# A four-layer diffusion block on one core: two top-k steps moved from VectorE to ScalarE and GpSimd, Newton steps of three instructions, projections at half pace in some phases

## What is computed

```python
scores = jnp.einsum('bqhd,bkhd->bhqk', q, k) / jnp.sqrt(jnp.float32(D))
top_s, top_i = jax.lax.top_k(scores, TOPK)          # TOPK = 16 of 77 keys
attn = jax.nn.softmax(top_s, axis=-1)
vg = jnp.take_along_axis(v_bh[:, :, None, :, :], top_i[..., None], axis=3)
o = jnp.einsum('bhqk,bhqkd->bqhd', attn, vg).reshape(B, L, C)
```

## Time and profile before

| what | value |
|---|---|
| median of 3 runs | 2932.87 us (2932.09 to 2951.3) |
| the profiled execution's own time | 2946.59 us |
| its span, first to last instruction | 2945.2 us |
| PE, PEld busy | 2444.7 us (83%), 1246.7 us |
| DVE busy | 1811.3 us (62%) |
| ACT busy | 1253.7 us (43%) |
| POOL busy | 258.6 us (9%) |
| granted TensorE clock, mean | 0.898 |

### The profile page before, as it was taken

One profiled execution on the slowest core, in us unless ns is written; L12 is line 12 of the kernel. 1 busy time (PEld: TensorE's weight loads), 2 busy tenths in 40 slices (PEclk: granted clock), 3 DMA queues, 4 the chain that ended last, 5 costly groups with the idle time before them and its releaser, 6 DMA issues.

```text
span 2945.2 us, 37122 instructions
## 1 busy us (share of the span) xinstructions
PE 2444.7 (83%) x13127; PEld 1246.7 (42%) x13127; DVE 1811.3 (62%) x5631; ACT 1253.7 (43%) x2346; POOL 258.6 (9%) x252
## 2 busy tenths in 40 slices
PE   6678667878797878999779999978879888899478
PEld 2455234544454444444344445442334332334235
DVE  5656867686434565557667666657776577774344
ACT  2323324433221213545325555535656626666234
POOL 2001000011210100000110010010010010010201
PEclk8799688889898878999889999988999979999768
DMA  4555222000000130000222100133120122100210
GB/s 159 165 129 175 74 87 69 17 21 7 4 8 25 58 70 12 12 22 21 88 81 82 41 15 12 37 104 96 38 42 12 65 81 73 33 22 8 72 41 15
DMA packets 151645, 161.30 MB, mean 55 GB/s; under 512 B 33471, under 2 KB 120978, under 8 KB 151196
## 3 DMA queue, kind: packets, MB, share of 16 engines
q1 hardware_dynamic: 151460, 158.94, 18.9%
HBM read 98.04 MB, written 60.19 MB: 54 GB/s over the span
## 4 chain that ended last, share of the span: by engine, by line
PE 63%; DVE 21%; ACT 6%; DMA 4%; issue 3%; POOL 2%; SPq 2%; DVEq 0%; ACTq 0%; POOLq 0%
PE bank L1104 9%; PE bank L1573 7%; PE bank L1076 7%; PE bank L1051 6%; PE bank L1594 5%; PE bank L2047 3%; PE bank L1080 3%; PE bank L731 3%; DVE max L1177 3%; PE bank L1493 2%; PE bank L2224 2%; DVE bank L1174 2%; DVE k_stack L1341 2%; PE bank L2049 2%; PE bank L672 1%
## 5 line engine op out<-in xcount | busy, mean ns | idle before, releaser
L1118 ACT ACTIVATE work<-bank 128x512 f32<-128x512 f32 (+1 forms) x1216 | 701.0, 597 | 643.6 <-PE bank L1080 290.1
L1174 DVE CUSTOM_DVE_ANT_0 bank<-bank,weights 128x512 f32<-128x512 f32 x512 | 349.2, 702 | 205.2 <-PE bank L1051 203.7
L1051 PE MATMUL bank<-k_stack,q_stack 97*128 97x512 bf16 x896 | 366.2, 412 | 79.5 <-DVE max L1174 38.1
L1177 DVE TENSOR_REDUCE max<-bank 128x1 f32<-128x512 f32 x512 | 341.0, 685 | 137.0 <-PE bank L1051 135.0
L1076 PE MATMUL bank<-q_stack,k_stack 99*128 99x512 bf16 x896 | 347.3, 390 | 17.9 <-ACT work L1118 13.3
L1573 PE MATMUL bank<-hT,weights 128*128 128x512 f32 x512 | 268.4, 624 | 21.3 <-ACT hT L693 7.8
L1080 PEld LDWEIGHTS bank<-ident_b,weights 128*128 128x128 bf16 x2048 | 160.7, 99 | 121.2 <-issue 14.2
L1051 PEld LDWEIGHTS bank<-k_stack,q_stack 97*128 97x128 bf16 x896 | 90.3, 101 | 286.3 <-DVE max L1174 113.9
L1080 PE MATMUL bank<-ident_b,weights 128*128 128x128 bf16 x2048 | 201.8, 221 | 0.0
L1594 PE MATMUL bank<-weights,work 128*128 128x256 f32 x768 | 196.7, 384 | 1.0 <-DVE work L1647 1.0
L1418 POOL TENSOR_TENSOR x<-x,work 128x512 f32<-128x512 f32 x64 | 82.0, 1281 | 1300.0 <-DVE work L1407 1296.6
(11 more groups left out here) (238 smaller groups left out, 3663.3 us busy)
## 6 DMA issues: line engine op xcount, KB each, us to landing
q_stack<-parts_q SPq DMA_DIRECT2D x60, 384.0 KB, 3.9
parts_q<-parts SPq DMA_DIRECT2D x46, 384.0 KB, 2.6
k_stack<-parts_k SPq DMA_DIRECT2D x40, 384.0 KB, 5.0
weights<-parts_q SPq DMA_DIRECT2D x36, 384.0 KB, 3.8
parts_q<-parts SPq DMA_DIRECT2D x46, 256.0 KB, 2.9
parts_k<-parts SPq DMA_DIRECT2D x24, 384.0 KB, 2.5
parts_k<-parts SPq DMA_DIRECT2D x24, 256.0 KB, 2.9
weights<-in_L_e_w SPq DMA_DIRECT2D x12, 512.0 KB, 5.7
```

Of the source, the lines that this page charges most:

```text
L1051: m = pe.e.matmul(bank.ap[:, :], self.q(g)[0:MAX_ROW, h, qt * P:(qt + 1) * P], k_stacks[self.key, g].ap[0:MAX_ROW, h, half * BLK:(half + 1 ...
L1118: ac.e.activation(p.ap[0:self.nk, :], banks[self.key, "exp", g, i].ap[0:self.nk, :], ACT.Exp).then_inc(*probs.tick((self.key, g, i)))
L1174: ve.e.tensor_tensor_reduce(bank[:, :], bank[:, :], mask_bias[:, qt, half * BLK:(half + 1) * BLK], 1.0, -3.4e38, ALU.add, ALU.max, to).the ...
L1177: ve.e.tensor_reduce(to, bank[:, :], AX_X, ALU.max).then_inc(*maxima.tick((self.key, g, i)))
```

## The change

- Top-k: the negated maxima (L1330) are made by an ACT instruction (Copy with scale -1) just ahead of the item's exponentials. The multiplication by the mask (L1348) leaves DVE; GpSimd makes a mask in place (`is_equal`) and multiplies the exponentials by it. PE's transposition and the buffer's release now wait for GpSimd.
- Roots: a Newton step has three instructions in place of four (two of them `scalar_tensor_tensor`).
- `Parts` gets a `pace`. With pace 2 an item takes four beats, and DVE's instructions for it are spread over them. It is given to `k` and `q` of b 1 in layer 0, `xq` of b 0 in layer 0, and `k2` and `q2` of both b in layer 2. Elsewhere pace is 1 and the order within a stage is as before.
- Window attention: the transposition and the division come two beats later (`late` 3), with two beats more for the stage.
- Last phase: the rows for half 1 are loaded at the head of its own lane rather than at the end of the phase before, and the rows of the cross output projection after the cross attention rather than ahead of it.

```diff
+        def newton_step(ve, key, y, v, w, n):
+            ve.e.tensor_tensor(w, y, y, ALU.mult).then_inc(*vec.tick((key, "root", n)))
+            ve.wait_ge(*vec[key, "root", n])
+            ve.e.scalar_tensor_tensor(out=w, in0=w, scalar=-0.5, in1=v, op0=ALU.mult, op1=ALU.mult).then_inc(
+                *vec.tick((key, "root", n + 1)))
+            ve.wait_ge(*vec[key, "root", n + 1])
+            ve.e.scalar_tensor_tensor(out=y, in0=w, scalar=1.5, in1=y, op0=ALU.add, op1=ALU.mult).then_inc(
+                *vec.tick((key, "root", n + 2)))
...
             def vector(self, ve):
+                yield from rest(2 * self.pace)
                 for c, bl in self.items:
+                    if self.pace == 1:
+                        for _ in self.split(ve, c, bl):
+                            pass
+                        yield from rest(2)
                     else:
+                        yield from self.split(ve, c, bl)
+
+            def split(self, ve, c, bl):
+                if self.rope:
...
+                    ve.e.tensor_tensor(r.ap[:, :], r.ap[:, :], sinT, ALU.mult).then_inc(*vec.tick((k, "sin")))
+                    yield
+                    ve.wait_ge(*vec[k, "sin"])
+                    ve.wait_ge(*pool_done[k, "cos"])
+                    ve.e.tensor_tensor(t, t, r.ap[:, :], ALU.add).then_inc(*vec.tick((k, "sum")))
...
+                    ve.e.tensor_copy(p.ap[:, 0, :], t).then_inc(*vec.tick((k, "p0")))
+                    yield
...
+                ve.e.tensor_tensor(t, t, p.ap[:, 0, :], ALU.subtract).then_inc(*vec.tick((k, "r1")))
+                if not self.rope:
+                    yield
+                ve.wait_ge(*vec[k, "r1"])
+                ve.e.tensor_copy(p.ap[:, 1, :], t).then_inc(*vec.tick((k, "p1")))
+                yield
+                ve.wait_ge(*vec[k, "p1"])
+                ve.e.tensor_tensor(p.ap[:, 2, :], t, p.ap[:, 1, :], ALU.subtract).then_inc(*vec.tick((k, "p2")))
+                yield from rest(1 if self.rope else 2)
...
+                self.late = 3 if kind == "window" else 1
+                self.beats += self.late - 1
...
-                s_left.take(n % 2, k, (vec, (k, "kept")))
+                s_left.take(n % 2, k, (pool_done, (k, "kept")))
...
-                pe.wait_ge(*vec[k, "kept"])
+                pe.wait_ge(*pool_done[k, "kept"])
...
+                            ac.wait_ge(*vec[k, "top", 0, TPB - 1])
+                            ac.e.activation(top8[k].ap[:, :, 2, 0:1], top8[k].ap[:, :, 0, 0:1], ACT.Copy, scale=-1.0).then_inc(
+                                *probs.tick((k, "low")))
+                            ac.wait_ge(*probs[k, "low"])
                             ac.wait_ge(*vec[k, "left", 0, TPB - 1])
...
+            def pool(self, po):
+                for beat in range(self.beats):
+                    if now := self.group(beat, 5, 16):
+                        if now[1] % 4 == 0:
+                            u, g = self.at(now[0])
+                            k = (u.key, g, now[1] // 4)
+                            left, ex = s_left[k].ap, s_exp[k].ap
+                            po.wait_ge(*vec[k, "left", 1, TPB - 1])
+                            po.wait_ge(*pool_done.latest)
+                            po.e.tensor_scalar(left[:, 1, :, :], left[:, 1, :, :], TAKEN, None, ALU.is_equal).then_inc(
+                                *pool_done.tick((k, "taken")))
+                            po.wait_ge(*pool_done[k, "taken"])
+                            po.wait_ge(*probs[k, TPB - 1])
+                            po.wait_ge(*pool_done.latest)
+                            po.e.tensor_tensor(ex[:, :, :], ex[:, :, :], left[:, 1, :, :], ALU.mult).then_inc(
+                                *pool_done.tick((k, "kept")))
+                    yield
...
-                    ve.wait_ge(*vec[k, "top", 0, TPB - 1])
-                    ve.e.tensor_scalar(top.ap[:, :, 2, 0:1], top.ap[:, :, 0, 0:1], -1.0, None, ALU.mult).then_inc(*vec.tick((k, "low")))
...
-                        ve.e.scalar_tensor_tensor(out=ex[:, :, :], in0=left[:, 1, :, :], scalar=TAKEN, in1=ex[:, :, :],
-                                                  op0=ALU.is_equal, op1=ALU.mult).then_inc(*vec.tick((k, "kept")))
...
-            return Rows(so), [so, n8, xq] + ([cross, Rows(co)] if blk is None else [Rows(co), cross]) + [co, n9, mlp, Store(b, mlp)], mlp.rows_left()
+            return Rows(so), [so, n8, xq, cross, Rows(co), co, n9, mlp, Store(b, mlp)], mlp.rows_left()
...
-            (of(1, "self3"), [rows_0] + last_0 + [rows_11]),
-            ([rows_10] + last_10, last_11),
+            (of(1, "self3"), [rows_0] + last_0),
+            ([rows_10] + last_10, [rows_11] + last_11),
```

More of the change, by code:

```diff
@@ L710, in __init__ @@
                 self.items = [(c, bl) for c in range(CC) for bl in self.blocks]
-                self.beats = 2 * len(self.items) + 2
+                self.beats = 2 * pace * (len(self.items) + 1)
             def stored(self, c):
@@ L733, in tensor @@
                         if i == 0:
-                            yield
+                            yield from rest(self.pace)
                     m.then_inc(*dense.tick(k))
-                    yield
+                    yield from rest(self.pace)
             def scalar(self, ac):
@@ new lines, in split @@
+            def split(self, ve, c, bl):
+                k = (self.key, c, bl)
+                t, p = work[k, "t"].ap[:, :], part_slots[k]
+                if self.rope:
+                    r = work[k, "r"]
+                    for f in r.free:
+                        ve.wait_ge(*f)
+                    ve.wait_ge(*evac[k, "t"])
+                    ve.e.stream_shuffle(r.ap[:, :], t, SHUFFLE).then_inc(*vec.tick((k, "shuffled")))
+                    ve.wait_ge(*ld_rope["all"])
+                    ve.wait_ge(*vec[k, "shuffled"])
+                    ve.e.tensor_tensor(r.ap[:, :], r.ap[:, :], sinT, ALU.mult).then_inc(*vec.tick((k, "sin")))
+                    yield
+                    ve.wait_ge(*vec[k, "sin"])
+                    ve.wait_ge(*pool_done[k, "cos"])
+                    ve.e.tensor_tensor(t, t, r.ap[:, :], ALU.add).then_inc(*vec.tick((k, "sum")))
+                    for f in p.free:
+                        ve.wait_ge(*f)
+                    ve.wait_ge(*vec[k, "sum"])
+                    ve.e.tensor_copy(p.ap[:, 0, :], t).then_inc(*vec.tick((k, "p0")))
+                    yield
+                    ve.wait_ge(*vec[k, "p0"])
+                else:
+                    ve.wait_ge(*evac[k, "p0"])
+                ve.e.tensor_tensor(t, t, p.ap[:, 0, :], ALU.subtract).then_inc(*vec.tick((k, "r1")))
[7 more added lines that the diff above has]
+                yield from rest(1 if self.rope else 2)
@@ L1031, in tensor @@
                             self.pv(pe, now[0], now[1] // 4)
-                    if now := self.group(beat, self.fin_at + 1, 1):
+                    if now := self.group(beat, self.fin_at + self.late, 1):
                         g = now[0]
@@ L1125, in vector @@
                 for beat in range(self.beats):
-                    if now := self.group(beat, self.fin_at + 2, 1):
+                    if now := self.group(beat, self.fin_at + self.late + 1, 1):
                         self.finish_out(ve, now[0])
@@ L2599, in build_program @@
         top_last = two_["topk", 1].key
-        topk_left = [(turned, (top_last, 3, n)) for n in range(2, 4)] + [(vec, ((top_last, 3, 3), "kept"))]
+        topk_left = [(turned, (top_last, 3, n)) for n in range(2, 4)] + [(pool_done, ((top_last, 3, 3), "kept"))]
         topk_first = TopK(of(0, ("topk", 0)), last_win)
```

68 lines of the change are left out of this document (17 added, 51 removed).

## The result

The changed kernel takes 2870.06 us (2864.85 to 2878.13, four runs) against 2938.28 us (2932.09 to 2951.3, four runs) of the kernel before beside it: a ratio of 0.9763, interval 0.9729 to 0.9798. In a second comparison, on another chip, it was 0.974 [0.9713, 0.9768]. That is faster by 70 to 76 us where 45 were forecast; 2870 lies inside the range of 2860 to 2930, near its fast end. The profiled execution took 2869.71 us, span 2868.4; its mean granted clock is 0.912 (before 0.898).

The account below looks back on a forecast made before the run. PE (83% busy) was taken to bound the whole, DVE to be full in `topk_first`. Terms 14 + 7 + 10 + 8 + 5 + 1 = 45 us off 2946.6, times 0.9953, gave 2888 us; range 2860 to 2930.

Parts of the forecast that it names:

- rival B: Top-k: GpSimd's port lock holds DVE instructions and eats the relief; 27 us gained in all, 2908 scaled; chance 0.12.
- Top-k, forecast 14: Top-k phases: DVE relieved of 42 us, 31 net; 5 us gained in `topk_first`, 9.5 in `topk_rest`, 14 in all.
- I take no net cost there: Top-k: GpSimd's later kept values cost PE's transposition, three beats behind, nothing net; bounds 0 and 83 us.
- 70% and 40%: Shares of DVE's net relief taken to reach the end: 70% in `topk_first` (5 us), 40% in `topk_rest` (9.5 us).
- GpSimd against DVE, forecast 11 us of loss: Top-k phases: a quarter of about 110 second-lane DVE instructions meet GpSimd and lose 0.4 us each, 11 us.
- rival C: Top-k: late kept values become the path; if all 64 turns wait, 83 us lost, 2985 scaled; chance 0.12.
- the forecast's own sign: Top-k: PE's waits for kept values, now under GpSimd, would be no longer in sum than 26.8 us.
- Roots, forecast 7: Norms: three fewer DVE instructions a call over 28 calls, 17 us of DVE, 7 us gained; bounds 0 and 17.
- Rotated projections, forecast 10 + 8: `k2` and `q2`: spreading DVE's work fills PE's idle time, 10 us for b 1's `k2`, 8 for b 0.
- One sign: Rotated projections: DVE's wait at L786 for GpSimd's cosine product would be gone from the profile.
- Projections without rotation, and the window finish, forecast 5 in all: Window attention phases: spread splits, later stores and later window transposition gain 5 us; bounds 0 and 12.
- Last phase, forecast 1: Last phase: row loads moved behind the attention gain 1 us; bounds -3 and 2.

Follow-up runs that it names:

- the later transposition: The changed kernel with PE's transposition of the kept values, the copy behind it and each top-k group's end one beat later: 2864.45 us, ratio 0.9733 to the kernel before.
- the load experiment: The changed kernel with a third GpSimd instruction per item behind the product, on data nobody reads: 2868.64 us, ratio 0.9749 to the kernel before.
- the longer mask: The changed kernel with one more GpSimd instruction per item, multiplying the mask by itself ahead of the product: ratio 0.9836 to the kernel before.

## Why the prediction held, and where its terms were off

*The direction and the mechanism.* Right: the forecast case, with DVE's relief reaching the end in the phases that DVE fills, is what the part alone shows. The total of 45 us was too small, against 66 of the five parts alone (16 + 16.5 + 25 + 8 + 0.6) and 70 to 76 of the whole; what lies between is within the errors of five ratios. The range held because it was wide: 2870 is 10 us from its fast end. Two of the sums don't come out as written: rival B's 27 us give 2906 scaled, not 2908, and the terms' lower bounds taken half give a slow end of about 2915, not 2906.

*Top-k, forecast 14, measured 16 (19.0 by phases).* The total held because errors cancelled. First, the relief was read too small. "L1330 costs the 0.08 us to the next start" leaves out what stands ahead of it, for it needs the last maximum:

```profile
305.30 0.65 DVE L1328 MAX8 top<-bank 128x8 f32<-128x77 f32 x4
```

From the start of the last of these four MAX8 to the next foreign instruction it is 0.34 us with L1330 between, and 0.145 without it in the changed kernel (medians of 64). So the negation costs DVE 0.20 us an item, 12.5 us in all, and the relief is some 50 us, not 42. Its move gave 10.3 us.

Second, "I take no net cost there" was wrong for GpSimd's latency. From the last replacement to the kept values it is now some 2.0 us instead of 0.6, and PE waits for them 11 us more (42.7 against 31.8).

Third, 70% and 40% were too low for the relief itself: with the product's move PE waits 13 us more and the phases are still 9.0 shorter, so some 22 of its 37 us arrived before that cost, an estimate from the waits. How much would arrive if the latency were none is not shown, as the later transposition took 17 us of these waits away and gave nothing back.

Mask and product were sized well, 0.976 and 0.834 us for the 0.8 and 0.83 taken, and so was ACT's negation, 0.21 us for the 0.25; the exponentials start only 0.06 us later behind the first replacements than before, so its cover held.

*GpSimd against DVE, forecast 11 us of loss.* Next to nothing of it is seen. In the two top-k phases 13 DVE instructions took over 0.08 us more than their line's median, 4.9 us in sum, against 8 with 3.7 us before. Small instructions that took 0.5 us and more are 3, not dozens, the longest 0.83 us. 45 us more of GpSimd's work cost about 1 us of the phases in the load experiment. Rival B is out. What DVE mostly does there is not held: none of the 154 MAX8 and 101 replacements that began inside a mask or product instruction of GpSimd was longer for it. The Trainium skill, page "SBUF — State Buffer", section "Who interferes with whom", has a DVE instruction with two SBUF inputs contend with a GpSimd instruction that reads SBUF. The trace agrees for GpSimd's product and not for its mask, which has one input; the chain of a root beside both:

```profile
382.40 0.98 POOL L1353 TENSOR_SCALAR k_stack<-k_stack 128x308 f32<-128x308 f32 x1 [4.35 <-DVE newton L590]
...
382.89 0.16 DVE L595 SCALAR_TENSOR_TENSOR rstd<-newton,rstd 128x4 f32<-128x4 f32 x1
...
383.46 0.83 POOL L1358 TENSOR_TENSOR k_stack<-k_stack 128x308 f32<-128x308 f32 x1
383.49 0.83 DVE L595 SCALAR_TENSOR_TENSOR rstd<-newton,rstd 128x4 f32<-128x4 f32 x1
```

The first L595 keeps its 0.16 us inside the mask; the second ends with the product.

*Kept values on the path, rival C.* Its mechanism is real and its size wrong. PE waits for kept values 18 times, 42.7 us, not the more than 40 times that would have made it true. But the forecast's own sign, that these waits are no longer than the 26.8 us before, failed: read in the same way they grew from 31.8 us to 42.7. And the waits aren't the whole cost: with the longer mask they grew by 11 us and the phases by 17.

The Trainium skill, page "GPSIMD Engine Reference", opening section, calls GpSimd the wrong choice for elementwise arithmetic, as DVE does it about twice as fast. The rows have GpSimd slower still, 0.976 + 0.834 us in two instructions for what DVE did in one of 0.48. Its advice doesn't follow for this place: where DVE is the full engine, the slower copy was worth 9.0 us of two phases.

*Roots, forecast 7, measured 16.5 (10 to 23).* This is the term that was missed by most. The working had the 17 us of DVE right and then took two fifths of it, since the roots stand in the norm's chain "in most, not all, norms". The wait for that chain shrank by 12 us by itself, from the 108.8 of the earlier trace rows, and `topk_first`, which DVE fills, gave 2.4 us.

*Rotated projections, forecast 10 + 8, measured 24.* The 8 for b 0 became 9.3. The 10 for b 1's four `k2` items became 17.5 in the whole of self2 b0: the upper bound named, 12.65 of idle time and another 6 for the clock, against 11.3 and 6.2. So the idle time was sized well, and the step that was off is the clock's part, which was named and then put at nothing. The waits named went (PE from 1339 us to self2 b1's start at 1505 before and 1448 after; us, times, longest):

```profile
PE bank L1051 <- DVE max L1174: 15.3, 7, 5.4
```

```profile
PE bank L1072 <- DVE max L1195: 2.0, 5, 1.0
```

No wait behind L1195 is over 3 us, as forecast. The maxima stand between an item's pieces, as DVE's timeline of the changed kernel has it (start, us), where the earlier trace rows had 5.8 us in one piece:

```profile
1376.90 0.79 DVE L793 STREAM_SHUFFLE work<-work 128x512 f32<-128x512 f32 x1
1377.72 0.69 DVE L796 TENSOR_TENSOR work<-work,weights 128x512 f32<-128x512 f32 x1
1378.33 0.69 DVE L1195 CUSTOM_DVE_ANT_0 bank<-bank,weights 128x512 f32<-128x512 f32 x1
...
1379.64 0.69 DVE L800 TENSOR_TENSOR work<-work 128x512 f32<-128x512 f32 x1
```

One sign failed in part. The wait of DVE for the cosine product (L786, now L800) did not go: 16 waits of 1.2 us before, 19.6 us, and now

```profile
DVE work L800 <- POOL work L771: 12.8, 11, 1.2
```

It went where two row maxima of the other lane came between the pieces, as in the timeline above, which is so in three of the four `k2` items of b 1. In nine of the eleven waits nothing of the other lane stands between the pieces, seven of these in b 0; in the other two something shorter than two maxima does. With 1.2 us at most each, none of these waits shows behind PE's own waits above.

*Projections without rotation, and the window finish, forecast 5 in all.* The later finish alone gives 8 us (4 to 12) and the paces alone nothing. The sum is within its bounds of 0 to 12, but the forecast laid it mainly on the spread of the split, and that is the wrong one of the two.

*Last phase, forecast 1.* Measured 0.6. In the profile the phase is 16.6 us shorter. Half of that, 8.1 us, is idle time of PE, and every kernel with the rows moved has as little of it. The other half is busy time, and that is not this edit: the kernel with top-k alone, whose last phase is unchanged, has the phase 10.2 us shorter too. Windows of the last phase, before and with top-k alone:

```profile
2688.30:2945.20 256.90, 187.38 (x828) 104.98 (x826) 97.84 (x254) 101.63 (x176) 33.21 (x38) 0.80 0.14 39
```

```profile
2668.60:2915.20 246.60, 174.68 (x827) 99.96 (x825) 97.39 (x254) 100.99 (x176) 33.20 (x38) 0.86 0.14 40
```

Idle time of PE is nearly the same (69.5 and 71.9 us); what differs is busy time, 12.7 us, at clock 0.80 and 0.86. So a part of the 77 us between the two profiles is luck of one execution; the medians decide.

## What to carry to other kernels

An instruction moved to a slower engine has two prices, and they are measured apart: put extra work ahead of the result that is waited for, then behind it; here the first cost 17 us of the two phases and the second 1. Count the waits for a result by its own end and the waiter's start: the engine that a row names was another in 7 of 18 cases. What an instruction costs its queue is the distance from the start of the one ahead to the start of the one behind, with it and without it; here that was 0.20 us where 0.08 had been read. In a phase that one engine fills, count small serial chains on it at well over half their length (here a root's three instructions, 17 us in all, gave 10 to 23), all the more where a chain heads a stage and the next engine has nothing else in its list. Where a burst of one lane's work stands before the instruction that PE waits for, cutting the burst into pieces gave PE's idle time back and some of its clock.

## What the runs showed of the hardware

The granted clock in the last phase is not fixed by the instruction stream. Both the kernel before and the one with top-k alone run the same instructions there, and in both PE stands 16.2 or 16.3 us at the head of cross attention. From within that wait on, the clock was at the level of 1.2 GHz for 51 us before, and for 27 us with top-k alone; the kernel before, then two stretches of the other (windows, columns as above):

```profile
2790.00:2830.00 40.00, 24.65 (x157) 11.55 (x158) 15.64 (x40) 11.26 (x19) 5.77 (x8) 0.50 0.39 96
```

```profile
2785.00:2805.00 20.00, 15.34 (x122) 7.43 (x125) 11.64 (x32) 10.42 (x19) 0.00 (x0) 0.76 0.21 56
2805.00:2825.00 20.00, 15.97 (x119) 7.00 (x112) 9.20 (x26) 12.56 (x23) 0.72 (x1) 1.00 0.20 54
```

The last phases differ by 10 us by it, a third of a per cent of the kernel. What decides between them, no run here tells.

On GpSimd a comparison with one input took longer than a product of two at the same size of 128 x 308: 0.976 against 0.834 us. The number of inputs alone doesn't set its time; a product and a difference whose two inputs are the same tile took 0.70.

The mask did not hold DVE's two-input instructions either: in the changed kernel three of them began more than 0.4 us into a mask instruction (root steps of 0.16 us, a difference of 0.69 us), and each took its usual time, while one that began 15 ns into a mask took 0.44 us instead of 0.17 and one beside the product 0.83.
